# A fused delta-rule and mixture-of-experts kernel with its eight looped steps written out, its chain semaphores left uncleared, its up weights loaded earlier from two engines, and its orders redrawn

## What is computed

```python
x = x + _L0_conv_ref(_ln_c(x), Wq, Wk, Wv, Wb, Wo)        # 12 heads of 16
t = _to_tokens(x)
t = t + _L0_ffn_ref(_ln_t(t), router_w, w_gate, w_up, w_down, ws_gate, ws_up, ws_down, sg_w, sg_b)
x = _from_tokens(t, x)
...
# inside the first: q, k = l2norm(silu(t @ Wq)), l2norm(silu(t @ Wk)); v = silu(t @ Wv); beta = sigmoid(t @ Wb)
# delta rule over the 256 tokens of each image and head, a 16 x 16 state S:
u_t = beta_t * (v_t - S_{t-1}^T k_t);  S_t = S_{t-1} + k_t u_t^T;  o_t = S_t^T q_t
# then out = t + o @ Wo
...
# inside the second: 8 experts of 192, all computed, the two best weighted; a shared expert of 768
g = jax.nn.silu(jnp.einsum('bsd,edh->bseh', x, w_gate)); u = jnp.einsum('bsd,edh->bseh', x, w_up)
expert_out = jnp.einsum('bseh,ehd->bsed', g * u, w_down)
shared = jax.nn.silu(x @ ws_gate) * (x @ ws_up) @ ws_down
return alpha * shared + (1.0 - alpha) * routed
```

## Time and profile before

| | us |
|---|---|
| median of 3 runs | 538.85 |
| lowest and highest | 537.14, 539.02 |
| the profiled execution | 535.79 |
| its span on the core | 534.1 |
| first recurrence instruction (chunk 0) | 30.55 |
| chunk 1 begins | 75.71 |
| chunk 2 begins | 104.75 |
| last recurrence instruction ends (chunk 15) | 488.03 |

### The profile page before, as it was taken

How to read it: one execution, slowest core, us unless ns; L and a number is a source line. 1 busy time by engine, 2 the same in 40 slices (tenths; PEclk the granted TensorE clock), 3 DMA queues, 4 the chain that set the end, 5 groups by cost and what they waited for, 6 DMA issues and landing times.

```text
span 534.1 us, 11599 instructions
## 1 busy us (share of the span) xinstructions
PE 439.0 (82%) x2464; PEld 384.2 (72%) x2464; DVE 435.6 (82%) x2546; ACT 330.8 (62%) x927; POOL 410.9 (77%) x525
## 2 busy tenths in 40 slices
PE   1552025799999999799979999899999998989996
PEld 0431013579888888688877978698988897979996
DVE  4177078999999999899979997999999999999300
ACT  2680053658585858485847767485858584746853
POOL 4471099989898989789895989698989899987341
PEclk9996555589999999999999999999999999999999
DMA  3659933232323222222222232313232323210300
GB/s 86 192 128 184 189 110 106 75 79 78 91 67 83 74 84 75 75 77 73 74 68 52 64 86 68 84 59 95 61 89 68 83 76 86 72 60 2 104 2 16
DMA packets 44682, 44.01 MB, mean 82 GB/s; under 512 B 19857, under 2 KB 36433, under 8 KB 44625
## 3 DMA queue, kind: packets, MB, share of 16 engines
q1 hardware_dynamic: 44624, 43.44, 31.2%
HBM read 37.13 MB, written 6.29 MB: 81 GB/s over the span
## 4 chain that ended last, share of the span: by engine, by line
DVE 65%; PE 10%; issue 6%; POOL 6%; SPq 6%; DMA 3%; ACT 1%; DVEq 1%; POOLq 0%; ACTq 0%
DVE Pr L1150 14%; DVE bank L1154 14%; DVE u L1152 14%; DVE SH L1158 12%; PE bank L421 3%; POOL PQ L778 3%; DMA W_unsplit<-in_L_ffn_ws_up_dram 2%; POOL PQ L785 2%; DVE st L907 2%; SPq L247 1%; DVE ss L991 1%; SPq L241 1%; PE bank L409 1%; SPq L246 1%; DVE mv L908 1%
## 5 line engine op out<-in xcount | busy, mean ns | idle before, releaser
L823 POOL TENSOR_TENSOR hid<-sg,ug 128x192 f32<-128x192 f32 x192 | 109.8, 598 | 39.4 <-ACT ug L611 36.9
L1150 DVE TENSOR_TENSOR Pr<-SH,bank 128x96 f32<-128x96 f32 x512 | 106.1, 251 | 17.8 <-ACT Pr L555 10.6
L778 POOL TENSOR_TENSOR PQ<-SH,QB 128x768 f32<-128x768 f32 x62 | 112.6, 1838 | 0.9 <-DVE SH L1158 0.9
L1154 DVE TENSOR_TENSOR bank<-bank,u 128x96 f32<-128x96 f32 x512 | 108.9, 261 | 0.0
L785 POOL TENSOR_TENSOR PQ<-PQ 128x768 f32<-128x768 f32 (+2 forms) x93 | 103.2, 1109 | 6.0
L1152 DVE TENSOR_REDUCE u<-Pr 128x6 f32<-128x102 f32 x512 | 107.7, 254 | 0.0
L421 PE MATMUL bank<-Wd,hidT 128*128 128x192 f32 x576 | 106.6, 326 | 0.0
L1158 DVE TENSOR_TENSOR SH<-SH,bank 128x96 f32<-128x96 f32 x512 | 106.2, 252 | 0.0
L421 PEld LDWEIGHTS bank<-Wd,hidT 128*128 128x128 f32 x576 | 93.7, 190 | 0.0
L610 ACT ACTIVATE sg<-bank 128x192 f32<-128x192 f32 x192 | 63.1, 329 | 44.1 <-PE bank L401 31.0
L358 PE MATMUL bank<-KR,Sel 128*128 128x384 f32 x128 | 55.1, 435 | 39.3 <-DMA KR<-k_scratch 25.6
(11 more groups left out here) (146 smaller groups left out, 816.3 us busy)
## 6 DMA issues: line engine op xcount, KB each, us to landing
QB<-q_scratch SPq DMA_DIRECT2D x64, 384.0 KB
k_scratch<-khl SPq DMA_DIRECT2D x64, 48.0 KB, 2.6
KR<-k_scratch SPq DMA_DIRECT2D x32, 96.0 KB, 2.4
q_scratch<-qn SPq DMA_DIRECT2D x64, 24.0 KB, 1.6
Wd<-in_L_ffn_w_down_dram SPq DMA_DIRECT2D x1, 1152.0 KB, 12.7
out_dram<-xT SPq DMA_DIRECT2D x1, 896.0 KB, 4.1
Wlo_unsplit<-in_L_ffn_w_gate_dram SPq DMA_DIRECT2D x1, 768.0 KB, 5.4
Wlo_unsplit<-in_L_ffn_w_up_dram SPq DMA_DIRECT2D x1, 768.0 KB, 7.9
```

What stands on the lines that cost most here:

```text
L778: tt(PQ[:, at * BR * HP:(at + n) * BR * HP].rearrange("p (i b h) d -> p i b (h d)", i=n, b=BR), SH[:, lo:lo + n].rearrange("p i b h d -> p ...
L823: tt(hid[:, r * H:(r + 1) * H], sg[:, m % RING], ug[:, m % RING], ALU.mult).then_inc(s_hid, 1)
L1150: v = each(lambda br: count(tt(Pr[:, br, i, :, 0:D], prev[:, br], KB[:, br], ALU.mult)), Sb)
L1154: v = each(lambda br: count(tt(KB[:, br], KB[:, br], u[:, i % 2, br].unsqueeze(2).to_broadcast([P, HP, D]), ALU.mult)), v)
```

## The change

`chunks` writes all 22 steps out. No chain semaphore is cleared any more, so DVE's wait for the whole count at the end of a step is gone too. The wait of a chunk's first product on the last state of the chunk before it is now carried over in `state`. `load_up` can be called by any engine: raw0 is issued by ACT in its step -3, behind the first `A_xs`; raw1 is issued by SP in `load`, in the place where raw0 stood; `load_later` keeps the rest of x and `Wd`. The tables of PE, ACT, POOL and the slots of DVE are redrawn.

```diff
-        def chunks(eng, step):
-
-            for c in range(-3, 4):
+        def chunks(step):
+
+            for c in range(-3, NC + 3):
                 step(c, c % 2)
-            with eng.Fori(0, 4) as k:
-                for j in range(2):
-                    step(eng.snap(k * 2 + (4 + j)), j)
-            for c in range(12, NC + 3):
-                step(c, c % 2)
...
+        def load_up(eng, i, to, lo, hi):
+
+            for half, we, ws in ((0, w_gate, ws_gate), (H, w_up, ws_up)):
+                eng.dma_start(to[:, 0:E, half:half + H], we[:, lo:hi, :].rearrange("e c h -> c e h")).then_inc(s_wu[i], 16)
+                eng.dma_start(to[:, E:UN, half:half + H], ws[lo:hi, :].rearrange("c (s h) -> c s h", h=H)).then_inc(s_wu[i], 16)
...
-                load_up(0, raw0, 0, C0)
+                load_up(sp, 1, raw1[0:C1], C0, C)
+                load_up(sp, 1, raw1[C1:P], C0, C)
 
             def load_later():
 
                 load_x(1, FIRST * T, L)
-                load_up(1, raw1[0:C1], C0, C)
-                load_up(1, raw1[C1:P], C0, C)
...
-                if n[0]:
-                    act.sem_clear(s_act)
-                    n[0] = 0
...
+                once(c, -3, load_up, act, 0, raw0, 0, C0)
...
-                if n[0]:
-                    pool.sem_clear(s_pool)
-                    n[0] = 0
...
+                at(0, summing, 0)
+                at(2, A_kn)
...
-                    at(14, 2, A_low)
-                    at(20, 2, A_z)
-                    at(23, -1, Fa_otok)
-                    at(31, 3, A_stats)
...
+                    at(11, 2, A_low)
+                    at(11, 1, A_vT)
+                    at(12, -3, Fc_res)
+                    at(15, 2, A_z)
+                    at(21, -1, Fa_otok)
+                    at(29, 3, A_stats)
...
-                    Sb = [None, None]
+                    Sb = state
...
-                        Sb = each(grow, v)
+                        Sb = state[:] = each(grow, v)
                         others(slot + 3)
-
-                if n[0]:
-                    dve.wait_ge(s_chain, n[0])
-                if running:
-                    dve.wait_ge(s_pair, c * 8 + 8)
-                if n[0]:
-                    dve.sem_clear(s_chain)
-                n[0] = 0
```

More of the change, by code:

```diff
@@ L293, in _ @@
             load()
-            chunks(sp, step)
+            chunks(step)
             sp.wait_ge(s_outc, NC)
@@ L636, in table @@
                 def table(n, name):
-                    if (not isinstance(n, int) or 0 <= n < NC) and tables[0] != name:
+                    if (0 <= n < NC) and tables[0] != name:
                         nc.scalar.preload_act_table_set(name)
                         tables[0] = name
-                if n[0]:
-                    act.sem_clear(s_act)
-                    n[0] = 0
                 at = partial(stage, c, par)
+                at(-3, hidden, 0)
+                at(-3, unit, 7)
@@ L646, in step @@
+                at(-3, unit, 8)
+                at(0, place, 0)
+                once(c, 1, weights_hi1, 5)
+                once(c, 0, weights_hi0, 5)
+                at(-2, Fa_h)
+                at(-3, unit, 9)
+                at(-3, hidden, 1)
+                at(-2, Fa_hT)
                 at(-3, unit, 10)
+                table(c + 1, LN_EXP)
+                at(1, A_inv)
+                at(-3, hidden, 2)
                 table(c - 2, LN_EXP)
                 at(-2, Fa_exp)
-                at(0, place, 0)
@@ L650, in step @@
-                table(c + 1, LN_EXP)
-                at(1, A_inv)
                 table(0, SILU)
-                at(-3, hidden, 2)
+                at(2, A_h)
                 at(-3, unit, 11)
-                once(c, 1, weights_hi1, 4)
+                at(-3, hidden, 3)
                 at(-2, unit, 0)
-                at(2, A_h)
+                once(c, 1, weights_hi1, 6)
                 at(2, A_xh)
+                at(-3, hidden, 4)
+                at(-2, unit, 1)
+                once(c, 0, weights_hi0, 6)
@@ L703, in step @@
-                at(-3, Fc_out)
-                once(c, 1, weights_hi1, 11)
-                at(-2, unit, 9)
+                at(0, place, 1)
             nc.scalar.preload_act_table_set(SILU)
@@ L710, in _ @@
             act.wait_ge(s_const, 4)
-            chunks(act, step)
+            chunks(step)
         @block.gpsimd
@@ L792, in summing @@
             def summing(c, p, half):
-                if half == 1 and isinstance(c, int) and c == NC - 1:
+                if half == 1 and c == NC - 1:
                     return
@@ L892, in _ @@
             pool.wait_ge(s_const, 4)
-            chunks(pool, step)
+            chunks(step)
         @block.vector
```

227 lines of the change are left out of this document (105 added, 122 removed).

## The result

The changed kernel takes 514.18 us (median of four runs, 511.73 to 514.96) against 538.61 before: a ratio of 0.9546 with a 95% interval from 0.9514 to 0.9578. That is 24.4 us faster, where 32.2 were forecast. The forecast of 506.7 had a range up to 516, so the time lies inside it, but near its upper end, and 8 us have to be accounted for.

A forecast was written before the change was run, and what follows sets the result against it. DVE was taken as the limit from chunk 2 on, waiting in chunks 0 and 1, with PE limiting the tail. Terms -12.0 - 2.4 - 12.4 - 4.9 + 1.0 - 1.5 = -32.2 gave 506.7 us, range 498 to 516.

The forecast's parts named there:

- Loop, -12.4: Chunks 3 to 11: writing out the looped steps removes turn gaps and register work on DVE, 12.4 us less.
- Clearing, -4.9: Chunk ends 2 to 14: without DVE's whole-count wait and clear, 0.38 us less at each of 13, 4.9 in all.
- The margins of 0.3 and 0.4 us: Full chunk: POOL's oT ready 0.3 us and PE's projection 0.4 us before DVE needs them, so no wait forecast.
- the rival of new waits: Chunk ends: POOL or PE is late, a full chunk stays at 26.8 us; +4.9, 511.6 us; chance 0.15.
- The slower rival: Slot 15: PE carries work over, its projection late each chunk; three units' worth gives 543 us; chance 0.04.
- Chunk 0's begin, +2.5: Start: Wp sharing DMA engines with raw0 and keys queued behind raw1 delay chunk 0 by 2.5 us (0 to 5).
- Chunk 1's begin, -12.0: Start: rs wait goes, a wait of some 5 us on keys replaces it; chunk 1 begins at 63.7, 12.0 us less.
- the start is a queue: Start: raws, Wp and chunk 0's keys collide, chunk 1's keys come at 68; +4.5, 511.2 us; chance 0.13.
- by its rate, 12.8 us less: Start: one working for chunk 1's keys, taking raw1 out of the loads ahead of them; the other gave 16.3 less.
- Chunk 1, -2.4: Chunk 1: POOL has 5 us more, so waits for oT shrink; 26.6 us instead of 29.04, 2.4 less.
- Chunk 2, +1.0: Chunk 2: PE at 1.2 GHz through chunk 1, zc at slot 15 waits for slow units; +1.0 us (0 to 3).
- Tail, -1.5: After the last recurrence: earlier fourth down group and PE up to two units ahead; 1.5 us less (0 to -3).

The follow-up runs named there:

- unroll_only: The kernel before with looped steps 4 to 11 written out; clears, loads and orders as before: 525.43 us against 538.82.
- keys01_res: keys1_res with raw1 issued behind chunk 0's keys and queries: 508.34 us.
- raw0_later: The changed kernel with ACT's issue of raw0 one step later, behind the second A_xs: 518.43 us.
- old_tables: The changed kernel with all orders of PE, ACT, POOL and DVE's slots as before: 509.02 us.
- res_behind: The changed kernel with DVE's res behind otok in the steps of the tail: 509.43 us.
- loads_only: The kernel before, its loop, clears and orders kept, with only the raw0 and raw1 loads moved: 527.51 us.
- keys1_first: The changed kernel with the rest of x and Wd issued behind chunk 1's keys and queries on SP: 505.96 us.
- keys1_res: The changed kernel with the edits of keys1_first and res_behind together: 502.39 us.
- old_keys1: old_tables with the rest of x and Wd issued behind chunk 1's keys: 501.28 us, ratio to before 0.9312.

## Why the prediction came out as it did

**Loop, -12.4: right.** `unroll_only` gave -13.4 by the medians, and its chunks 3 to 11 took 241.53 us against 241.4, 12.2 less than before.

**Clearing, -4.9: right, a little too large.** 4.15 us measured. The distance across a chunk end is 0.39 us, within the 0.33 to 0.40 forecast; a chunk takes 26.48 us, not 26.4. The margins of 0.3 and 0.4 us held: in chunks 5 to 11 of the changed kernel no wait of DVE for PE or POOL is over 0.3 us. So neither the rival of new waits nor the slower one came. But the old orders hold too, so that question did not depend on the tables. The slower rival's price was also wrong: three units of 0.85 us are 2.55 us, under the 2.7 from which it would be slower, and give 536.8, not 543. **Chunks 12 to 15** were to give 1.1 and gave 0.4 and 0.5; chunk 12 took 26.83 us with the redrawn orders and 26.49 with the old ones.

**Chunk 0's begin, +2.5: measured +3.8.** Two terms stood in it. "Wp now shares the DMA engines with raw0: 0 to 2" was too small: it was 4.3 (14.9 against 10.6). "raw1 then stands in SP's queue ahead of chunk 0's keys" was the weight of my 2.5, and `keys01_res` shows it cost nothing as the kernel stands. `raw0_later` shows that the keys are delayed once `Wp` is on time, by raws under way: by the order on SP's queue, as I had it, or by the full engines. I had added two delays that hide each other. The Trainium skill (DMA: Bandwidth & Descriptors, Queues, rings and completion order) says that a DMA engine takes turns between the queues it has work for, packet by packet. By that, a large load on a second queue takes its share from a small urgent one on the first, and the trace agrees: 0.6 MB of `Wp` landed 4.3 us later.

**Chunk 1's begin, -12.0: measured -7.9 and -8.8.** Its mechanism was right: the wait for `rs` went, the keys behind `Wd` came, and the rival that I called "the start is a queue" (keys at 68, 0.13) describes it best: 67.8 and 66.9. The step that failed is "so Wd is in at 54.2 and the readback can go out a little later, at 55". It went out at 63.95. I counted 2.2 MB of queries and x from 35 us on; the first `QB` was issued at 34.94 only, so all 2.75 MB were still to come, and the rest of x and `Wd` went out from 37.56 on. And I gave `Wd` the 246 GB/s of one stretch of before. From 40 to 60 us the stretches of the changed kernel show 150 to 230, of which two:

```profile
45.00:50.00 5.00, 1.38 (x2) 0.57 (x2) 4.96 (x31) 2.49 (x6) 5.00 (x7) 1.00 1.04 150
50.00:55.00 5.00, 1.37 (x2) 0.57 (x2) 4.96 (x30) 2.22 (x6) 4.92 (x3) 1.00 1.03 218
```

The lower of two rates in the rows was the safe one: queries, x and `Wd` are 4.5 MB, and at 182 GB/s from 38 on they are in at 62.7, near the 63.1 that was seen. So was the other of my two workings, "by its rate, 12.8 us less": with the measured 3.8 of chunk 0 it gives 66.7.

**Chunk 1, -2.4: measured -1.5**; POOL was busy for 26.21 of its 27.51 us, and which of its work was late was not tried. **Chunk 2, +1.0 with the clock at 1.2 GHz:** PE was at that level in chunk 1 in both profiles, as expected (0.56 in the second, and by its durations in the first). Chunk 2 took 26.38 and 26.79 us, 0.2 less and 0.2 more than before; with the 0.4 that the missing clear gives, slow units cost 0.2 and 0.6 us, not 1.0.

**Tail, -1.5: wrong in sign, +0.9 and +3.7.** This is the one term whose mechanism failed. The step is "chunk 15's otok, which comes no sooner after the end than before". It comes later: 8.3 us after the end, where it was 5.7. I had followed `Fc_res` from slot 36 to 12 in a full chunk, where it costs nothing; in the steps of the tail there are no tokens between the slots, so slot 12 is simply ahead of slot 21, and what waits there holds `otok`. That the idle PE then also lost its clock was not in the range for the tail at all.

**The redrawn orders as a whole** stood in the sum with -1.5 in the tail and +1.0 in chunk 2, and cost 5.2 us by the medians. Everything else in the sum was -31.7 and measured -29.8 (`old_tables`). The forecast was thus good for the other three parts, and wrong on the one that moved most lines.

**Luck.** The range reached 516 because two rivals were added up in it. One of them came, the queue at the start; new waits at the chunk ends did not, and the tail, which no rival priced, took their room. That 514.2 lies inside is in part luck.

**What stays open.** With the same start, chunk 1 began at 64.99 (`res_behind`), 65.26 (`old_tables`), 66.90 and 67.83 (the changed kernel) and 67.74 (`loads_only`); `Wd` held SP for 15.0 to 17.4 us in these profiles and the keys behind it took 7.0 to 8.3 us more, and no run tells why it varies. So a difference of 1 to 2 us between two medians with this start is weak evidence; with the keys in front (`keys1_first`, `keys1_res`, `old_keys1`) chunk 1 began at 59.60 to 59.72 in all three profiles, and there the comparison is firmer. Nor do the runs show why the clock fell behind the same wait in three profiles and not in the fourth. Whether the queue's order or the full engines delay the keys was not separated, and a start in which `Wp`, both raws and chunk 0's keys are all on time was not found.

## What to carry to other kernels

A table of slots that interleaves small work with a long recurrence becomes a plain list in the steps where the recurrence doesn't run: read every moved line there too, and keep what the last result needs ahead of all that waits. Put small transfers that the next stage needs ahead of large ones that are needed late. A large early load on a second queue took 4.3 us from a small urgent one here, but moving it later cost 4.3 us in all: look at what the load will meet instead. Where a change has several parts, time it with each part taken out: here the smallest-looking parts, the loop and three lines on SP, were worth more than all redrawn orders, which cost.

## What the runs showed of the hardware

- An issue took longer where the DMA engines were full: `Wd`'s two transfers held SP for 16.8 us in the changed kernel (share of the engines 0.96 to 1.04 from 40 to 55 us) and for 3.8 us when they were issued 15 us later, in a stretch at 0.36; eight issues of raw1 held ACT's own work for 8.25 us. The Trainium skill (DMA: Bandwidth & Descriptors, Issuing engines are not separate DMA queues) calls the time to initiate a transfer usually small beside the transfer itself. Here the page of the profile gives 20.5 us from issue to landing for `Wd`'s first part, and 9.15 of them were the issue; the measurement decides.
- A wait of PE of 1.94 or 1.95 us in the tail was followed, in three of the four profiles that have it, by some 7 us at the 1.2 GHz level. In the changed kernel that was worth about 2.8 us, more than the wait itself.
- The granted clock can read 1.00 where a trace doesn't show a lower level: in chunk 1 of the first profile a multiplication took 522 ns, in chunks 3 to 11 338 ns. The durations are the check.
- A turn of a hardware loop cost some 3.15 us on DVE at each of the three turns (3.84 to 3.92 against 0.73), and the profile put it down to another engine's instruction.
